# The last turn of a cross-attention also prepares the self-attention that follows it, both in one block

## What is computed

```python
# cross-attention of layer 0 (context 512 rows for each sequence)
q = einsum(layernorm(x), wq); k, v = einsum(ctx, wk), einsum(ctx, wv)
attn = softmax(q k^T * SCALE); attn = where(mask == 0, 0, attn)
x = x + reshape(swap(attn v)) @ proj_w + proj_b
# self-attention of layer 0 (16 heads of 32)
q, k, v = (layernorm(x) @ W + b for each of Wq, Wk, Wv), split in heads
q, k = q @ Wp, k @ Wp                      # the same 32x32 matrix for every head
x = x + softmax(q k^T / sqrt(32)) v
# MLP of layer 0 with weights +1 and -1 (2048, 2048, 512)
h = layernorm(x); h = relu(s0 * h' @ k0) * 2; h = relu(s1 * h @ k1) * 2; x = x + s2 * h @ k2
# layer 1: another cross-attention, a rotary self-attention, a quantized MLP
```

## Time and profile before

| what | value |
|---|---|
| median of 3 runs | 1225.25 us (1223.09 to 1227.37) |
| profiled execution, its own time | 1227.47 us |
| its span, first to last instruction | 1225.7 us |
| TensorE busy | 1110.3 us (91%) |
| VectorE, ScalarE, GpSimd busy | 577.9, 378.0, 193.3 us |
| mean granted TensorE clock | 0.961 of full |

### The profile page before, as it was taken

How to read it: one execution, slowest core, us unless ns; L and a number is a source line. 1 busy time by engine, 2 the same in 40 slices (tenths; PEclk the granted TensorE clock), 3 DMA queues, 4 the chain that set the end, 5 groups by cost and what they waited for, 6 DMA issues and landing times. The chain is left out here.

```text
span 1225.7 us, 17854 instructions
## 1 busy us (share of the span) xinstructions
PE 1110.3 (91%) x6507; PEld 684.4 (56%) x6528; DVE 577.9 (47%) x998; ACT 378.0 (31%) x1012; POOL 193.3 (16%) x184
## 2 busy tenths in 40 slices
PE   8999988999899999999998999957998999994986
PEld 4544437887444444444443755446696868773542
DVE  2232016777743231511112544256938475658766
ACT  1211125666321010301101222244413233236864
POOL 0012001333213230000000112025122121300004
PEclk9999998999899999999999899979999999996999
DMA  9964702001001100000006777740000000007001
GB/s 341 387 229 170 288 1 78 2 1 35 26 26 34 43 9 1 1 0 0 0 1 232 272 268 269 304 167 5 1 1 0 0 0 0 0 0 283 1 1 69
DMA packets 55128, 108.61 MB, mean 89 GB/s; under 512 B 4144, under 2 KB 4528, under 8 KB 55088
## 3 DMA queue, kind: packets, MB, share of 16 engines
q1 hardware_dynamic: 55088, 108.09, 24.6%
HBM read 105.98 MB, written 2.10 MB: 88 GB/s over the span
## 5 line engine op out<-in xcount | busy, mean ns | idle before, releaser
L1643 ACT ACTIVATE f_act<-bank,f_sgn 128x512 f32<-128x512 f32 x64 | 44.0, 687 | 270.1 <-PE bank L1598 270.1
L1598 PE MATMUL bank<-f_a_lo,f_w 128*128 128x512 f16 x512 | 115.7, 379 | 0.0
L1598 PE MATMUL bank<-f_a_hi,f_w 128*128 128x512 f16 x512 | 115.7, 379 | 0.0
L1675 DVE CAST f_b_hi<-f_act 128x512 f32 x32 | 25.5, 795 | 166.2 <-ACT f_act L1643 166.2
L1598 PEld LDWEIGHTS bank<-f_a_lo,f_w 128*128 x512 | 50.1, 98 | 60.4
L1598 PEld LDWEIGHTS bank<-f_a_hi,f_w 128*128 x512 | 50.1, 98 | 60.2
L527 POOL TENSOR_TENSOR x_mv<-x_mv,eps 128x2 f32<-128x2 f32 x8 | 1.5, 193 | 404.4 <-DVE x_mv L420 404.4
L276 PE MATMUL bank<-x_cT,x_qT 128*64 128x512 f32 x256 | 61.3, 625 | 0.0
L1448 DVE TENSOR_TENSOR s_e<-s_pair,s_tables 128x512 f32<-128x512 f32 x64 | 41.4, 687 | 42.0 <-POOL s_kT L1508 24.8
L514 DVE TENSOR_TENSOR xres<-bank,xres 128x512 f32<-128x512 f32 (+1 forms) x16 | 11.1, 692 | 105.3 <-PE bank L333 91.5
L295 PE MATMUL bank<-x_cN,x_eT 128*64 128x512 f32 x256 | 58.4, 610 | 0.0
(11 more groups left out here) (315 smaller groups left out, 2277.7 us busy)
## 6 DMA issues: line engine op xcount, KB each, us to landing
x_cT<-in_ctx_cols_dram SPq DMA_DIRECT2D x32, 1024.0 KB, 7.4
x_cN<-in_ctx_rows_dram SPq DMA_DIRECT2D x32, 1024.0 KB, 9.6
f_upper_bits<-in_f_w_dram SPq DMA_DIRECT2D x20, 256.0 KB, 2.7
f_raw<-in_f_wd_dram SPq DMA_DIRECT2D x1, 2816.0 KB, 17.6
x_qw<-in_x_qw_dram SPq DMA_DIRECT2D x8, 256.0 KB, 4.7
x_kw<-in_x_kw_dram SPq DMA_DIRECT2D x8, 256.0 KB, 5.5
x_vw<-in_x_vw_dram SPq DMA_DIRECT2D x2, 1024.0 KB, 14.6
s_wk_ahead<-in_s_wk_dram SPq DMA_DIRECT2D x1, 2048.0 KB, 14.3
```

The source lines that it names most:

```text
L1598: mm = pe.matmul(h_bank[s][:, :], weights(2 * i + s, k), part[:, k, cols], start=(n == 0 and k == 0), stop=(n == 1 and k == k_chunks - 1))
L1643: act.activation(act32[s][:, :], h_bank[s][:, :], ACT.Relu, scale=sgn[:, layer % 2:layer % 2 + 1]).then_inc(h_read, 1)
L1675: dve.tensor_copy(hi[:, 2 * i + s, :], act32[s][:, :]).then_inc(hhi_ok, 1)
```

## The change

1. x0 and s0 stand in one block; the end of phase between them is gone. The buffers that both use (`Front`: statistics, normalised rows, split transposed rows, with their semaphores) are allocated outside, and the counts on them run on from x0 to s0 (`FIRST`).
2. The preparation of s0 moves into the last turn of x0 (`HeadWeights`, called `following`): statistics, normalisation and transposition of the first two tiles as in the other turns; the square of `Wp` behind the transposition; the folded bias ahead of the transposition of the exponentials; two chunks of the query fold ahead of the attended context of s=0 and two behind it; the copies and splits on ScalarE and VectorE in between. The value weights are copied between ScalarE's two output copies.
3. SyncE issues the three weight tensors and the eight small transfers behind the last context of x0. The bits of the MLP and its scales are issued when the last residual of x0 is added (`x_done`); GpSimd clears `v_diag` behind the same wait, at the start of s0.
4. In f0 GpSimd gives the first credits, and its first conversions wait for other counts of `h_done`.
5. x1 gets its buffers from outside, with nothing following.

```diff
+    def load(self, sp):
+        io, rows = self.io, lambda w: w.rearrange("(c p) n -> p c n", p=P)
+        sp.dma_start(self.wqT[:, :, :], rows(io["s0_wqT"])).then_inc(self.raw_in, 16)
+        sp.dma_start(self.wk_raw[:, :, :], rows(io["s0_wk"])).then_inc(self.raw_in, 16)
+        sp.dma_start(self.wv_raw[:, :, :], rows(io["s0_wv"])).then_inc(self.raw_in, 16)
+        sp.wait_ge(self.set_ok, 1)
+        for g in range(4):
+            sp.dma_start(self.wpT[32 * g:32 * g + 32, 32 * g:32 * g + 32], io["s0_wpT"]).then_inc(self.small_in, 16)
...
+    def square(self, pe):
+        pe.wait_ge(self.small_in, 16 * 8)
+        pe.matmul(self.core.bank[4][:, 0:P], self.wpT[:, :], self.wpT[:, :], start=True, stop=True).then_inc(self.prep_pe, 1)
+
+    def fold_bias(self, pe):
+        pe.wait_ge(self.prep_dve, 1)
+        pe.matmul(self.core.bank[5][:, 0:KC], self.gram[:, :], self.bq_in[:, :], start=True, stop=True).then_inc(self.prep_pe, 1)
+
+    def fold(self, pe, cs):
+        for c in cs:
+            if c == 0:
+                pe.wait_ge(self.raw_in, 48)
+            elif c == 1:
+                pe.wait_ge(self.prep_dve, 2)
+            else:
+                pe.wait_ge(self.lo_ok, c - 1)
+            for j in range(KC):
+                mm = pe.matmul(self.core.bank[self.G_BANK[c]][:, j * P:(j + 1) * P], self.wqT[:, j, c * P:(c + 1) * P], self.gram[:, :],
+                               start=True, stop=True)
+            mm.then_inc(self.prep_pe, 1)
...
@@ cross_attention, sync @@
+            if following is not None:
+                following.load(sp)
@@ cross_attention, tensor, in turn(i, last) @@
-                    if s == 0 and not last:
+                    if s == 0 and (not last or following is not None):
                         transpose_x(i + 1)
+                    if s == 0 and last and following is not None:
+                        following.square(pe)
+                if last and following is not None:
+                    following.fold_bias(pe)
...
+                if last and following is not None:
+                    following.fold(pe, (0, 1))
...
+                    if s == 0 and last and following is not None:
+                        following.fold(pe, (2, 3))
...
+                    if last and following is not None:
+                        pe.wait_ge(xlo_ok, 2 * i + 4)
@@ cross_attention, scalar @@
+                elif following is not None:
+                    following.copy_queries(act, (0, 1))
+                    following.copy_raw(act, following.wk_hi, following.wk_raw)
...
+                    if s == 0 and last and following is not None:
+                        following.copy_queries(act, (2, 3))
...
+                        if s == 0 and last and following is not None:
+                            following.copy_raw(act, following.wv_hi, following.wv_raw)
@@ cross_attention, vector @@
+                elif following is not None:
+                    layernorm(0, i + 1)
...
-                    if s == 0 and not last:
+                    if s == 0 and (not last or following is not None):
                         split_x(i + 1)
+                    if s == 0 and last and following is not None:
+                        following.scale_square(dve)
...
+                if last and following is not None:
+                    following.keep_bias(dve)
+                    following.split_queries(dve, (0, 1), 0)
+                    following.split_raw(dve, following.wk_lo, following.wk_raw, following.wk_hi, 3)
+                    following.split_queries(dve, (2, 3), 3)
+                    following.split_raw(dve, following.wv_lo, following.wv_raw, following.wv_hi, 6)
@@ head_attention @@
         def _(sp):
-            sp.wait_ge(set_ok, 1)
...
+            sp.wait_ge(x_done, TILES + 2)
             for n in range(2):
                 sp.dma_start(sign_weights[1 + n][:, :, :], sign_weights[0][n, :, :, :].rearrange("c p h -> p c h")).then_inc(bits_in, 16)
+            sp.dma_start(scales_in[:, :], sign_weights[4].partition_broadcast(P)).then_inc(scales_loaded, 16)
...
-            transpose_x(0)
-            pe.wait_ge(small_in, 16 * n_small)
...
+            act.wait_ge(weights.prep_dve, 3)
+            act.wait_ge(x_done, TILES + 2)
...
-            rstd(0)
+            pool.wait_ge(x_done, TILES + 2)
             for v in v_diag:
                 pool.memset(v[:, :, :, :, :], 0.0).then_inc(set_ok, 1)
@@ sign_mlp, vector @@
-            dve.memset(core.spare[:, 0:1], 0.0).then_inc(h_read, 2)
-            dve.memset(core.spare[:, 1:2], 0.0).then_inc(y_read, 2)
-            dve.memset(core.spare[:, 2:3], 0.0).then_inc(hlo_ok, 2)
@@ sign_mlp, gpsimd @@
+            pool.memset(core.spare[:, 1:2], 0.0).then_inc(h_read, 2)
+            pool.memset(core.spare[:, 2:3], 0.0).then_inc(y_read, 2)
+            pool.memset(core.spare[:, 3:4], 0.0).then_inc(hlo_ok, 2)
             pool.wait_ge(var_ok, 2)
...
-                if f in range(1, 4):
-                    pool.wait_ge(h_done, 4 * f)
-                elif f:
+                if f < 4:
+                    pool.wait_ge(h_done, 4 * f + 3)
+                else:
                     pool.wait_ge(h_done, HC + f - 3)
```

More of the change, by code:

```diff
@@ L52, in end_phase, with __init__ @@
         self.sems = []
-def cross_attention(core, tag, ctx_rows, ctx_cols, qw, kw, vw, out_bias, scale, mask=None, proj=None,
-                    biases=None, clip=None, ahead=(), x=None, identity=None):
+class Front:
+    def __init__(self, core, stack, tag):
+        sb = lambda n, s, d=F32: core.sbuf(stack, f"{tag}_{n}", s, d)
+        self.stats = sb("stats", [P, 2, 6])
+        self.mv = sb("mv", [P, 2, 4])
+        self.xn = [sb(f"xn{s}", [P, D]) for s in range(2)]
+        self.xT_hi = sb("xT_hi", [P, KC, 2 * P], F32R)
+        self.xT_lo = sb("xT_lo", [P, KC, 2 * P], F32R)
+        self.stats_ok, self.var_ok, self.rstd_ok, self.xn_ok, self.xT_done, self.xhi_ok, self.xlo_ok = (
+            core.sem(stack, f"{tag}_{n}") for n in ("stats_ok", "var_ok", "rstd_ok", "xn_ok", "xT_done", "xhi_ok", "xlo_ok"))
@@ L67, in cross_attention @@
+def cross_attention(core, block, tag, front, qw_sb, kw_sb, m_hi, m_lo, ctx_rows, ctx_cols, qw, kw, vw, out_bias, scale, mask=None, proj=None,
+                    biases=None, clip=None, ahead=(), x=None, identity=None, following=None):
     nc = core.nc
@@ L141, in cross_attention @@
         vsplit = sem("vsplit")
[L142 to L148, removed]
+        stats_ok, var_ok, rstd_ok, xn_ok = front.stats_ok, front.var_ok, front.rstd_ok, front.xn_ok
+        xT_done, xhi_ok, xlo_ok = front.xT_done, front.xhi_ok, front.xlo_ok
         q_done = sem("q_done")
@@ L444, in row_constants @@
                 dve.wait_ge(dot_ok, 3 * n + 3)
+            if following is not None:
+                following.clear(dve)
             dve.memset(core.spare[:, 1:2], 0.0).then_inc(x_ok, 2)
@@ L538, in turn @@
             def turn(i, last):
-                if not last:
+                if not last or following is not None:
                     rstd(i + 1)
@@ L549, in _, with head_attention @@
             turn(TILES // 2 - 1, True)
-def head_attention(core, block, tag, heads, wq, wk, wv, bq, bk, bv, scale, wqT, wpT, ahead, sign_weights, sign_inputs, sign_scales):
+        return x_ok
+def head_attention(core, block, tag, heads, front, weights, x_done, sign_weights, sign_inputs, sign_scales):
     nc = core.nc
@@ L677, in transpose_signs, with project_transposed @@
                     mm.then_inc(fT_done, 1)
-            def project_transposed(banks, hi, lo, done, split):
-                pe.wait_ge(lo_ok, split)
+            def project_transposed(banks, hi, lo, done):
                 for g in range(2):
@@ L823, in turn @@
                 act.wait_ge(v_done, 2 * i + 1)
+                if first:
+                    act.wait_ge(set_ok, 1)
                 for b in range(2):
@@ L944, in turn @@
                 dve.wait_ge(v_done, 2 * i + 2)
+                if first:
+                    dve.wait_ge(set_ok, 2)
                 for b in range(2):
@@ L2124, in program @@
         on_chip = {n: core.sbuf(held, f"s1_w{n}_ahead", [P, KC, 2 * D]) for n in "kq"}
-        cross_attention(core, "x1", io["ctx_rows"], io["ctx_cols"], io["x1_qw"], io["x1_kw"], io["x1_vw"],
-                        io["x1_vb"], float(1.0 / np.sqrt(D).astype(np.float32)), biases=(io["x1_qb"], io["x1_kb"]), clip=100.0,
-                        ahead=[(rows(io[f"s1_w{n}"]), on_chip[n][:, :, :]) for n in "kq"])
+        with ExitStack() as st:
+            qw, kw = (core.sbuf(st, f"x1_{n}", [P, KC, D]) for n in ("qw", "kw"))
+            m_hi, m_lo = (core.sbuf(st, f"x1_{n}", [P, KC, D], F32R) for n in ("m_hi", "m_lo"))
+            front = Front(core, st, "x1")
+            block = st.enter_context(nc.Block())
+            cross_attention(core, block, "x1", front, qw, kw, m_hi, m_lo, io["ctx_rows"], io["ctx_cols"], io["x1_qw"], io["x1_kw"],
```

(2 more changed lines are left out.)

213 lines of the change are left out of this document (96 added, 117 removed).

## The result

The changed kernel took 1213.39 us (median of 4 runs, 1213.19 to 1213.72) beside 1224.17 us of the kernel before in the same measurement (4 runs, 1222.97 to 1227.37). The ratio is 0.9907, 95% interval 0.9881 to 0.9933: faster by 10.8 us, with 8.2 to 14.6 us inside the interval. Forecast were 9.2 us and 1216.1 us. The profiled execution took 1213.19 us for a span of 1211.4 us, 14.3 us less than the profiled span before. One thing is needed to read this: executions of one and the same program spread by up to 9.8 us in one measurement (the kernel before, 1218.21 to 1228.04 beside the later runs), and the profiled execution of before was one of the longer ones.

The account below looks back on a forecast made before the run. TensorE, busy 91% of the span, was taken as the bound, so only its standstills and low clock count. First seam 7.4 plus second 1.8 gave 9.2 us off 1225.25: 1216.1 us, range 1212.0 to 1219.8.

Parts of the forecast that it names:

- First seam: Between x0 and s0: all 16.9 us go, the last turn grows by 9.5, so 7.4 us saved.
- The stall for the normalised rows and the square: x0's last turn: TensorE's wait for normalised rows, priced by the third turn, costs 5.3 us; the square 0.4.
- The folded bias: x0's last turn, ahead of the transposes of s=0: cost 0, since TensorE idles there anyway; 0.4 without that cover.
- The folds and the wait in them: x0's last turn: four query-fold chunks on TensorE cost 3.6 us, and the second chunk's wait for VectorE 0.2.
- Beside the path: x0's last turn: ScalarE's and VectorE's copies and splits hide under TensorE's products at 0; at most 1 us if late.
- the small transfers come late: Rival: in x0's last turn the square waits for late small transfers, kernel 7.9 us slower, 1233; chance 0.04.
- The bits of the MLP: Issued after x0's last residual add, they land at 198.3, hidden with 0.9 us to spare before VectorE needs them.
- Second seam: Between s0 and the MLP: early credits start the fifth tile 3.95 us earlier, less 2.2 for the clock: 1.8 saved.
- no fall of the clock: Rival: at the second seam the clock stays full, saving 3.95 us instead of 1.8, total 1213.9; chance 0.15.
- All behind it only move: The MLP's other work, x1 and all stages behind only move; nothing for them in the 9.2 us sum.

Follow-up runs that it names:

- scores-first run: Changed kernel, with TensorE making both halves of the scores in x0's last turn before transposing the rows for s0: 1206.79 us, ratio 0.9864.
- The later conversion: Changed kernel, with GpSimd's first conversion in the MLP waiting for four hidden tiles instead of three: 1213.16 us, ratio 0.9890.
- second measurement: Changed kernel once more, unedited, against the kernel before: 1214.32 us beside 1226.51, ratio 0.9898.

## Why the prediction was right

**First seam: 7.4 forecast, 7.22 measured.** The last turn from its last residual add to the first projection: 40.85 forecast, 41.00 measured, and 40.9 to 41.0 in all six runs that keep this order. By terms:

- *The stall for the normalised rows and the square,* 5.3 + 0.4: second half of the scores at 7.24 + 0.4 = 7.64 behind the residual add; measured 7.61, then 4.67 for 4.78. Together 5.6 for 5.7. The clock is at 0.57 over the 3.2 us shown, much as in the earlier trace rows. It fell in all six profiles that have this stall, but the price leaned on it, and the second turn's wait of 1.40 us brings it down in three of thirteen only. The scores-first run removed the stall and got 5.5 back.
- *The folded bias* at 0: the transposes behind it still waited 0.80 for ScalarE. Right.
- *The folds and the wait in them,* 3.8: the pairs took 2.17 and 2.05 us, some 4.2. This 0.4 is the largest miss in the first seam's sum.
- *Beside the path:* ScalarE had been idle for 1.07 us when its second output copy was due, where 1.5 were forecast; no output product waited.
- *Small transfers:* the last of them was issued at 141.65 and landed 7.6 us later, at 149.3, and the square ran at 154.11. The rival "the small transfers come late" needed 9.2 us more than its due time; they had 4.9 to spare. But those of 2 and 4 KB took 7.6 to 8.9 us to land, behind 3 MB of weights, where the same ones took 1.6 to 1.9 at the old seam; the longest of the eight there, of 256 KB, took 3.0. The upper bound was 3.0 us for each, one after another, which was high enough only because it added them up.

**The bits of the MLP,** forecast hidden with 0.9 us to spare, had nothing to spare: the second landed 8.9 us after its issue, and VectorE's L992 (the chunk of the MLP's first weights, L931 before) waited 0.42 for it. It started 10.2 us after the first projection, where the forecast had 10.0, and s0 as a whole is 0.26 us longer.

**Second seam: 1.8 forecast, 2.04 measured** (2.0 to 2.4 over the runs). The fifth tile was forecast 10.3 us after the first, it came at 10.26; the stall 3.3, it was 3.17; the normalisation stayed at 2.57 beside GpSimd, as it had to by the 0.4 us between the third tile and GpSimd. The low clock lasted about 3.4 us, the lower end of the range of 3.0 to 6.0 that I had halved, and half of that is 1.7 back in place of 2.2. That term was set in the middle of a wide range, so its being near is in part luck. The rival "no fall of the clock" is refuted by the window, and TensorE slows down behind this stall in all six profiles that have it. The later conversion, with stalls of 1.61 and 0.96 us, kept the clock at full in its one profile. The Trainium skill, "TensorE: Matmul & The Clock Gate", section "HAM oscillation", has the clock fall in a wait that is long enough, and be won back after each such wait. The trace agrees in kind: the clock was lost and won back behind the stall of 3.17 us. But that stall is a little shorter than the section's rule asks for, and the clock also fell behind 1.51 + 0.75 us, and behind one wait of 2.30 us and not behind another; here the measurement decides.

**The sum** was 9.2 and the two seams give 9.3. The measured 10.8 (12.2 by the medians of the second measurement) holds 1.5 to 2.9 us more, of which the prediction knew nothing. "All behind it only move" was the step that fell short: the instructions only move, but the clock that they are granted is not the same in every profile. The kernel before reaches the shorter stages as well, with a delay of 1.2 us ahead of them, so that part isn't tied to the new code; that the change has no share in it isn't shown. It also widens what such a comparison can tell: 3.7 us, taken as the bound for no change, is less than the some 5 us between the two kinds of executions of the kernel before.

## What to carry to other kernels

A seam between two stages is priced best by a neighbour that has already been overlapped: the third turn gave the fourth turn's stall, clock and all, within 0.2 us. Then ask what the engine that waits could do first; moving TensorE's own later products, or VectorE's next splits, in front of the late data took another 5.5 and 4.3 us off these stages, since the low clock went with the stall. For effects of a few us compare the lengths of the touched stages as well as the totals, since total times of the same program differ by more.

## What the runs showed of the hardware that was not expected

- The clock's share in unchanged stages: x1, with the same 720 matmuls, took 152.7 to 156.7 us at granted clocks of 0.97 to 0.95, and 1.2 us of delay ahead of it went with a change in either direction (156.7 to 152.7 in the kernel before, 153.0 to 154.1 in the changed one).
- A short wait of TensorE may or may not bring its clock down: the wait of 2.30 us in x1 was followed by a clock of 0.58 in one profile and 1.00 in another, and that of 1.40 us in x0 by a fall in three of thirteen. A stall of 3.17 us was followed by one each time (0.52 over 3.4 us in the changed kernel).
- GpSimd beside VectorE stretched some of VectorE's work: two normalisations from 1.00 to 2.57 us, a cast from 0.42 to 2.12, a difference from 0.69 to 2.21. It didn't stretch all of it: the row maximum at 113.04 took 0.68 us under GpSimd's bias adds, and 0.69 at 159.39 in the changed kernel with GpSimd idle. Moving GpSimd moved the price.
- Transfers of 2 and 4 KB issued behind 3 MB of weights landed 7.6 to 8.9 us after their issue, where the same ones took 1.6 to 1.9 at the old seam.
